# Two-layer block (linear recurrence, then squared-ReLU feed-forward): another order of the VectorE, ScalarE and GpSimd calls of an inner batch

## The chip, the cores and the metric

The kernel runs on one core of one Trainium2 chip. The metric is the device time of one launch in microseconds. It was run three times: 826.71 us median, 822.82 us lowest, 884.32 us highest.

## What is computed

The input is 8 batches of 1024 tokens of width 512, in float32. Cut to what matters:

```
x = x + layernorm(attn(layernorm(x)))
x = x + layernorm(ffn(layernorm(x)))

attn(x):  s    = sigmoid(silu(x @ s_w1.T + s_b1) @ s_w2.T + s_b2)
          u    = (x @ B_w.T + B_b) * s
          h_t  = h_(t-1) @ A.T + u_t            (a scan over the 1024 tokens)
          y    = h @ C_w.T + C_b + x @ D_w.T + D_b
          return y * sigmoid(x @ g_w.T + g_b)
ffn(x):   square(relu(x @ Ws1)) @ Ws2 + routed  (routed is weighted by trunc(softmax weight): 0 unless a weight rounds to 1)
```

## The kernel before

A batch is 128 partitions by 8 tiles j of 128x512. Every operand of a large matmul is split into a high and a low part, and one product is three matmuls (`mm3`, lines 495 to 497: high by high, low by high, high by low). TensorE therefore has, for one inner batch, 396 matmuls of 512 columns, and between them 14 short matmul steps and one step of seven matmuls for the scan (`scan_step`, lines 531 to 539).

All engines run lists of calls written out by hand, one `tail` and one `body` for each batch; the order of the calls on an engine is its program, and engines meet only in semaphores. Batch 0 has a `first_tail`, the batches 1 to 6 a `tail`, the batches 0 to 6 a `body`, and batch 7 a `last_tail` and a `last_body`.

TensorE's `body` of batch b is: Y0 G4 Y1 G5 Y2 G6 Y3 G7 Y4 H00 H01 Y5 B0 SG0 Y6 W1f00 W1f01 Y7 W2(0) W2(1) W2(2) H10 H11 B1 SG1 W2(3). G is the gate of a tile, Y its output, H, B and SG make u of the next batch in two halves, W1f and W2 are the feed-forward in two halves. `tail` holds G0 to G3, the scan, and the second half of the feed-forward of the batch before.

What the prediction follows is the way from Y of a tile to W1f00 of the same batch, which needs tiles 0 to 3:

- VectorE `attn(j)` (line 1307) multiplies Y by the gate; `v_bn`, `v_ag`, `v_ep` (1312, 1316, 1320) take mean and variance; GpSimd `v_rs(j)` (1896) the power -1/2; VectorE `attn_norm(j)` (1324) normalizes.
- GpSimd `x1(j)` (1936) adds the residual. VectorE `x1_bn`, `x1_ag`, `x1_ep` (1329, 1333, 1337), GpSimd `x1_rs(j)` (1896, 1906), ScalarE `x1_norm(j)` (926) are the second norm.
- VectorE `turn(j)` (1347) transposes blocks of 32x32; the transfer queue's `move` (420) moves a pair of tiles by four transfers, after the turns of both; ScalarE `t_hi(j)` (917) and GpSimd `t_low(j)` (1947) split it.
- TensorE `W1f00` waits for `t_low(3)`, and for `u_of(0)` (VectorE, 1381), which frees the PSUM bank that it writes. `u_of(0)` waits for ScalarE's `s_gate(0)` (982), and that for SG0.

Beside it, the next batch's input is normalized on the same engines: a transfer broadcasts the statistics into `rows_in`; ScalarE `rows_apart(m)` (932) spreads a half of them; VectorE `less_mean(i)` and `scaled(i)` (1246) apply them to a pair of tiles; ScalarE `ft_hi(j)` (950) and VectorE `ft_low(j)` (1340) split. TensorE H00 waits for `ft_low(3)`, H10 for `ft_low(7)`. ScalarE `hs(j)` (901) and VectorE `hs_low(j)` (1300) split the state for Y(j). `h1` (1364, 1370) and `h1_low` (1953) make the hidden values that SG takes.

Of the kernel before, what the change touches and what calls it, by code (L numbers as in the profile page):

```python
# [18 lines left out]
def build(nc, x, xt, A, AT, BwT, Bb, CwT, Cb, DwT, Db, s1T, s1b, s2T, s2b, gwT, gb, Ws1p, Ws1, Ws2, W1, W2, Wr, eye, out):  # L19
# [19 lines left out]
    with ExitStack() as ctx:  # L39
# [830 lines left out]
        def _(eng):  # L870
# [128 lines left out]
            def tail(b, rep):  # L999
                a = (b, rep)  # L1000
                hidden(*a, 1, 0)
                gate(*a, 0)
                hidden(*a, 1, 1)
                hs(*a, 0)
                hs(*a, 1)
                gate(*a, 1)
                gate(*a, 2)
                zn(*a, 4)
                zn(*a, 5)
                gate(*a, 3)  # L1010
                zn(*a, 6)
                zn(*a, 7)

            def body(b, rep):
                a = (b, rep)
                hs(*a, 2)
                rows_apart(*a, 0)
                gate(*a, 4)
                ones_in(*a, 0)
                ft_hi(*a, 0)  # L1020
                hs(*a, 3)
# [39 lines left out]
                s_gate(*a, 1)  # L1061
                t_hi(*a, 6)
# [135 lines left out]
        def _(eng):  # L1198
# [276 lines left out]
            def tail(b, rep):  # L1475
# [49 lines left out]
                scan_add(*a, 14)  # L1525

            def body(b, rep):
# [3 lines left out]
                hs_low(*a, 2)  # L1531
# [11 lines left out]
                x1_bn(*a, 0)  # L1543
# [4 lines left out]
                hs_low(*a, 3)
                attn(*a, 2)
                x1_ep(*a, 0)  # L1550
                v_bn(*a, 2)
                x1_bn(*a, 1)
                v_ag(*a, 2)
                x1_ag(*a, 1)
                hs_low(*a, 4)
                x1_ep(*a, 1)
                v_ep(*a, 2)
                ft_low(*a, 2)
                turn(*a, 0)
# [11 lines left out]
                x1_bn(*a, 2)  # L1571
                attn(*a, 4)
                x1_ag(*a, 2)
                x1_ep(*a, 2)
                v_bn(*a, 4)
                x1_bn(*a, 3)
# [3 lines left out]
                v_ep(*a, 4)  # L1580
# [48 lines left out]
                x1_ep(*a, 7)
# [495 lines left out]
```

## Time and profile before

| what | us |
|---|---|
| median of the three runs | 826.71 |
| lowest, highest | 822.82, 884.32 |
| span of the profiled execution | 820.9 |
| TensorE (PE) busy in it | 789.0 |
| GpSimd (POOL) busy | 465.6 |
| VectorE (DVE) busy | 599.7 |
| ScalarE (ACT) busy | 346.7 |
| length of batch 2, first scan step to first scan step | 97.13 |

The page gives the span of the profiled execution, from its first instruction to its last; what lies around the span in that execution is not on the page. A row of a timeline names the start, the length, the engine, the line of the kernel, the operation and its tiles; in brackets stands how long the engine was idle before it and who released it. Times of the prediction are those of batch 2, in us from the start of the span.

### The profile page before, as it was taken

Reading aid. Unit: us, or ns where it says so; the run is one execution under the profiler, and the core shown is the slowest. Engines: PE = TensorE matmul, PEld = TensorE weight load, DVE = VectorE, ACT = ScalarE, POOL = GpSimd, SP = SyncE. Lnnn points to the kernel's source line nnn. Section 1 sums busy time; section 2 is a strip of 40 time slices with the busy share of each in tenths; the row PEclk is TensorE's granted clock in tenths of the full one; section 3 lists DMA queues with packets and bytes.
Section 4 is the critical chain, followed back from the end, with each engine's and each line's share of the span. In section 5 each row is a group of like instructions: output and inputs, shape, how many; then the busy total and the mean of one; then the engine's idle time right before and its main releaser. Section 6 shows DMA issues by size and latency. Waiting matters only on the chain. (4 is left out here: it accounts for less than half of the span.)

```text
span 820.9 us, 10797 instructions
## 1 busy us (share of the span) xinstructions
PE 789.0 (96%) x3644; PEld 650.4 (79%) x3644; DVE 599.7 (73%) x1393; ACT 346.7 (42%) x555; POOL 465.6 (57%) x560
## 2 busy tenths in 40 slices
PE   7989999999999999999999999999999999999985
PEld 6778878887888878888788887888788887888873
DVE  7858875697857977678775787578785797744774
ACT  4524435344433444344433544534443344432453
POOL 1243658438565576456574565844756557634555
PEclk9999999999999999999999999999999999999998
DMA  8524333544255424362334533354425522322112
GB/s 287 175 80 178 95 115 131 177 164 142 81 176 196 139 78 154 110 250 77 100 132 168 192 89 111 137 178 163 145 79 178 188 95 78 102 104 103 52 51 104
DMA packets 39614, 109.85 MB, mean 134 GB/s; under 512 B 6915, under 2 KB 23683, under 8 KB 31750
## 3 DMA queue, kind: packets, MB, share of 16 engines
q1 hardware_dynamic: 39126, 108.95, 39.4%
q8 instruction: 29, 0.48, 0.2%
q10 hardware_dynamic: 432, 0.20, 0.1%
q14 instruction: 27, 0.22, 0.1%
HBM read 60.84 MB, written 33.61 MB: 115 GB/s over the span
## 5 line engine op out<-in xcount | busy, mean ns | idle before, releaser
L1936 POOL TENSOR_TENSOR xres<-work,xres 128x512 f32<-128x512 f32 x64 | 83.1, 1299 | 65.1 <-DVE work L1324 65.1
L1896 POOL TENSOR_TENSOR rsv<-rsv,negh 128x1 f32<-128x1 f32 x64 | 53.3, 832 | 105.9 <-DVE rsv L1320 105.8
L495 PE MATMUL TM<-gw_hi,xT_hi 128*128 128x512 f32 x256 | 107.2, 419 | 0.0
L497 PE MATMUL TM<-gw_hi,xT_lo 128*128 128x512 f32 x256 | 100.7, 393 | 0.0
L497 PE MATMUL TM<-dw_hi,xT_lo 128*128 128x512 f32 x256 | 100.2, 391 | 0.0
L496 PE MATMUL TM<-gw_lo,xT_hi 128*128 128x512 f32 x256 | 100.1, 391 | 0.0
L495 PE MATMUL TM<-dw_hi,xT_hi 128*128 128x512 f32 x256 | 100.0, 391 | 0.0
L496 PE MATMUL TM<-dw_lo,xT_hi 128*128 128x512 f32 x256 | 99.6, 389 | 0.0
L987 ACT ACTIVATE work<-TM,nmz,rsz 128x512 f32<-128x512 f32 x62 | 48.2, 777 | 112.7 <-POOL nmz L1906 112.7
L1940 POOL TENSOR_TENSOR work<-work,xres 128x512 f32<-128x512 f32 x62 | 79.0, 1290 | 8.0 <-ACT work L987 8.0
L1246 DVE TENSOR_TENSOR xin<-xin,norm_row 128x1024 f32<-128x1024 f32 x56 | 71.2, 1305 | 11.4 <-ACT norm_row L932 11.4
L1947 POOL TENSOR_TENSOR x2T_lo<-work,x2T_hi 128x512 fp32r<-128x512 f32 x56 | 70.9, 1288 | 5.8 <-ACT x2T_hi L917 5.8
L926 ACT ACTIVATE work<-xres,nmx,rsx 128x512 f32<-128x512 f32 x64 | 54.5, 871 | 39.7 <-POOL nmx L1906 39.7
L1896 POOL TENSOR_TENSOR mv<-ve,negh 128x4 f32<-128x4 f32 (+1 forms) x17 | 17.9, 1051 | 82.9 <-DVE ve L1221 76.4
L495 PE MATMUL FM<-x2T_hi,f1w_hi 128*128 128x512 f32 x128 | 53.2, 415 | 11.7 <-POOL x2T_lo L1947 11.6
L1307 DVE TENSOR_TENSOR work<-TM,work 128x512 f32<-128x512 f32 x64 | 43.4, 678 | 24.8 <-PE TM L497 24.3
L917 ACT ACTIVATE x2T_hi<-work 128x512 fp32r<-128x512 f32 x56 | 33.7, 625 | 59.4 <-DMA work<-x2q 59.4
L1427 DVE BATCH_NORM_STATS2 st<-TM 128x6 f32<-128x512 f32 x62 | 42.7, 689 | 19.9 <-PE TM L497 19.9
L497 PEld LDWEIGHTS TM<-gw_hi,xT_lo 128*128 128x128 f32 x256 | 48.0, 188 | 10.9
L497 PEld LDWEIGHTS TM<-dw_hi,xT_lo 128*128 128x128 f32 x256 | 48.1, 188 | 10.1
L496 PEld LDWEIGHTS TM<-dw_lo,xT_hi 128*128 128x128 f32 x256 | 48.1, 188 | 9.9
L495 PEld LDWEIGHTS TM<-dw_hi,xT_hi 128*128 128x128 f32 x256 | 48.1, 188 | 9.8
(177 smaller groups left out, 2062.3 us busy)
## 6 DMA issues: line engine op xcount, KB each, us to landing
xres<-in_x SPq DMA_DIRECT2D x16, 1024.0 KB, 5.9
x_scratch<-xres SPq DMA_DIRECT2D x16, 1024.0 KB, 4.6
xin<-in_x SPq DMA_DIRECT2D x15, 1024.0 KB, 5.3
out<-work SPq DMA_DIRECT2D x30, 512.0 KB, 3.4
xin<-in_x_t SPq DMA_DIRECT2D x14, 1024.0 KB, 5.8
work<-x2q SPq DMA_DIRECT2D x112, 128.0 KB, 2.7
rows_in<-ln_scratch SPq DMA_DIRECT2D x14, 512.0 KB, 4.7
xin<-in_x SPq DMA_DIRECT2D x2, 512.0 KB, 5.1
```

The costliest lines, as they stand in the source:

```text
L495: eng.matmul(ps, lhs[0], rhs[0], start=first, stop=False)
L496: eng.matmul(ps, lhs[0], rhs[1], start=False, stop=False)
L497: return eng.matmul(ps, lhs[1], rhs[0], start=False, stop=last)
L926: eng.activation(dst, src, ACT.Identity, bias=nmx[:, j:j + 1], scale=rsx[:, j:j + 1])\
L987: eng.activation(work[:, j, :], z_bank(rep, j)[:, :], ACT.Identity, bias=nmz[:, j:j + 1], scale=rsz[:, j:j + 1]).then_inc(S["zn_ok"], 1)
L1246: return eng.tensor_tensor(xT, xT, r.unsqueeze(2).to_broadcast([P, 2, KD, P]), op)
L1307: eng.tensor_tensor(work[:, j, :], tm_bank(f"y{j}")[:, :], work[:, j, :], ALU.mult)\
L1427: eng.bn_stats(st6[:, 3, j, :], z_bank(rep, j)[:, :]).then_inc(S["z_bn"], 1)
L1896: return eng.tensor_tensor(dst, src, negh[:, 0:n], ALU.pow)
L1936: eng.tensor_tensor(xres[:, j, :], work[:, j, :], xres[:, j, :], ALU.add).then_inc(S["x1_ok"], 1)
L1940: eng.tensor_tensor(work[:, j, :], work[:, j, :], xres[:, j, :], ALU.add).then_inc(S["out_ok"], 1)
L1947: eng.tensor_tensor(by_blocks(x2T_lo[:, j % MS, :, :]), moved_tile(j), by_blocks(x2T_hi[:, j % MS, :, :]).bitcast(F32), ALU.subtract).then ...
```

## The change

The calls of ScalarE's, VectorE's and GpSimd's `tail` and `body` are put in another order. No call is added or taken away, and no call's instructions are changed. TensorE's list and the transfer queue's list stay as they are. `tail` is run by the batches 1 to 6, `body` by the batches 0 to 6.

```diff
 ScalarE, body
+                rows_apart(*a, 0)
                 hs(*a, 2)
-                rows_apart(*a, 0)
                 gate(*a, 4)
...
                 hs(*a, 3)
                 gate(*a, 5)
-                ft_hi(*a, 1)
+                rows_apart(*a, 1)
                 ft_hi(*a, 2)
+                x1_norm(*a, 0)
                 hs(*a, 4)
-                x1_norm(*a, 0)
-                rows_apart(*a, 1)
                 x1_norm(*a, 1)
...
+                t_hi(*a, 2)
+                s_gate(*a, 0)
+                t_hi(*a, 3)
                 hs(*a, 7)
...
 VectorE, body
-                less_mean(*a, 2)
-                turn(*a, 1)
                 attn(*a, 3)
                 v_bn(*a, 3)
+                hs_low(*a, 4)
+                v_ag(*a, 3)
+                less_mean(*a, 3)
+                v_ep(*a, 3)
+                x1_bn(*a, 2)
                 ft_low(*a, 3)
-                v_ag(*a, 3)
-                scaled(*a, 2)
-                v_ep(*a, 3)
-                less_mean(*a, 3)
+                x1_ag(*a, 2)
                 attn_norm(*a, 3)
...
                 turn(*a, 2)
                 h1(*a, 0, 0)
-                x1_ep(*a, 3)
+                turn(*a, 3)
+                x1_bn(*a, 4)
+                x1_ag(*a, 4)
                 h1(*a, 0, 1)
-                x1_bn(*a, 4)
-                turn(*a, 3)
                 attn(*a, 5)
...
 GpSimd, body
                 x1_rs(b, 2)
                 v_rs(b, 4)
+                x1_rs(b, 3)
                 x1(b, 4)
-                x1_rs(b, 3)
+                t_low(b, 1)
                 h1_low(b + 1, 0, 0)
                 h1_low(b + 1, 0, 1)
                 x1_rs(b, 4)
-                t_low(b, 1)
                 v_rs(b, 5)
```

In `tail`, GpSimd takes the second `ln1_rs` earlier, VectorE takes `scan_add(2)` and the statistics of the next input earlier and `hs_low(1)` last, and ScalarE takes `gate(0)` behind `hidden(1,1)` and `hs(0)`.

First place, VectorE in `body` around the turns of tiles 2 and 3. L1347 is a turn (the first of two is tile 2), L1337 the small step `x1_ep`, L1364 and L1370 are `h1`. Before:

```order
L1347 STREAM_TRANSPOSE x2q<-work 128x4x128
L1364 SCALAR_TENSOR_TENSOR hf<-FM0,b_col,hf 128x512
L1370 CAST h1_hi<-hf 128x512
L1337 TENSOR_SCALAR rsx<-mvx 128x1
L1364 SCALAR_TENSOR_TENSOR hf<-FM1,b_col,hf 128x512
L1370 CAST h1_hi<-hf 128x512
L1329 BN_STATS st6<-xres 128x6
L1347 STREAM_TRANSPOSE x2q<-work 128x4x128
```

And now, from `scaled(2)` (L1246) to the turn of tile 3:

```order
L1246 TENSOR_TENSOR xin<-xin,norm_row 128x1024
L1320 TENSOR_SCALAR rsv<-mvv 128x1
L1300 TENSOR_TENSOR hs_lo<-u,hs_hi 128x128
L1337 TENSOR_SCALAR rsx<-mvx 128x1
L1300 TENSOR_TENSOR hs_lo<-u,hs_hi 128x128
L1324 TENSOR_SCALAR work<-work,mvv,rsv 128x512
L1347 STREAM_TRANSPOSE x2q<-work 128x4x128
L1364 SCALAR_TENSOR_TENSOR hf<-FM0,b_col,hf 128x512
L1370 CAST h1_hi<-hf 128x512
L1347 STREAM_TRANSPOSE x2q<-work 128x4x128
```

`x1_ep(3)` stood behind the first `h1` and stands ahead of both turns; the turn of tile 3 stood behind both `h1` and an `x1_bn`, and stands between the two `h1`.

Second place, ScalarE in `body` around the second `rows_apart` (L932). L950 is `ft_hi`, L926 `x1_norm`, L901 `hs`, L892 `gate`. Before:

```order
L901 ACTIVATE hs_hi<-u 128x128
L892 ACTIVATE work<-TM2 128x512
L950 ACTIVATE xT_hi<-xin 128x512 x2
L901 ACTIVATE hs_hi<-u 128x128
L926 ACTIVATE work<-xres,nmx,rsx 128x512
L932 ACTIVATE norm_row<-rows_in 128x1024
L926 ACTIVATE work<-xres,nmx,rsx 128x512
```

And now:

```order
L950 ACTIVATE xT_hi<-xin 128x512 x2
L901 ACTIVATE hs_hi<-u 128x128
L892 ACTIVATE work<-TM2 128x512
L932 ACTIVATE norm_row<-rows_in 128x1024
L950 ACTIVATE xT_hi<-xin 128x512
L926 ACTIVATE work<-xres,nmx,rsx 128x512
L901 ACTIVATE hs_hi<-u 128x128
L926 ACTIVATE work<-xres,nmx,rsx 128x512
```

`rows_apart(1)` stood behind `ft_hi(2)`, `hs(4)` and `x1_norm(0)`, and stands ahead of them.

Third place, ScalarE in `body` from the norm of tiles 2 and 3 (L926) to `s_gate(0)` (L982). L917 is `t_hi`, L972 `sig`. Before, from the norm of tile 3:

```order
L926 ACTIVATE work<-xres,nmx,rsx 128x512
L917 ACTIVATE x2T_hi<-work 128x4x4x32
L892 ACTIVATE work<-TM0 128x512
L901 ACTIVATE hs_hi<-u 128x128
L901 ACTIVATE hs_hi<-carry 128x128
L939 ACTIVATE xin<-xin,one 1x4x128
L950 ACTIVATE xT_hi<-xin 128x512
L917 ACTIVATE x2T_hi<-work 128x4x4x32 x2
L950 ACTIVATE xT_hi<-xin 128x512
L982 ACTIVATE sg<-FM1,b_col 128x512
```

And now, from the norm of tile 2 to `hs(7)` (on carry):

```order
L926 ACTIVATE work<-xres,nmx,rsx 128x512
L917 ACTIVATE x2T_hi<-work 128x4x4x32
L926 ACTIVATE work<-xres,nmx,rsx 128x512
L972 ACTIVATE hf<-FM1,b_col 128x512
L917 ACTIVATE x2T_hi<-work 128x4x4x32
L982 ACTIVATE sg<-FM1,b_col 128x512
L917 ACTIVATE x2T_hi<-work 128x4x4x32
L901 ACTIVATE hs_hi<-carry 128x128
```

`s_gate(0)` stood behind `gate(7)`, two `hs`, `ones_in`, two `ft_hi` and the `t_hi` of tiles 2 and 3, and stands between the `t_hi` of tile 2 and of tile 3.

## Rows read from the trace of the kernel before

**Rows 1.** the page: span, and busy time of the engines

```profile
span 820.9 us, 10797 instructions
...
PE 789.0 (96%) x3644; PEld 650.4 (79%) x3644; DVE 599.7 (73%) x1393; ACT 346.7 (42%) x555; POOL 465.6 (57%) x560
```

**Rows 2.** waits of PE, whole span: line, released by, us in total, times, longest

```profile
PE FM L495 <- POOL x2T_lo L1947: 11.6, 7, 1.9
```

**Rows 3.** windows, batch 2: length, busy us of PE, PEld, DVE, ACT, POOL

```profile
229.23:326.36 97.13, 95.52 (x439) 78.81 (x438) 73.39 (x172) 42.16 (x67) 58.83 (x71) 1.00 0.43 141
```

**Rows 4.** timeline of PE in batch 2: start us, us, engine, line, operation

```profile
283.52 0.40 PE L495 MATMUL FM<-xT_hi,s1w_hi 128*128 128x512 f32 x1
...
296.50 0.39 PE L495 MATMUL TM<-dw_hi,xT_hi 128*128 128x512 f32 x1
...
299.69 0.40 PE L497 MATMUL TM<-cw_hi,hs_lo 128*128 128x512 f32 x1
...
301.70 0.50 PE L495 MATMUL FM<-x2T_hi,f1w_hi 128*128 128x512 f32 x1 [1.61 <-POOL x2T_lo L1947]
...
302.04 0.39 PE L496 MATMUL FM<-x2T_lo,f1w_hi 128*128 128x512 f32 x1
...
314.80 0.39 PE L495 MATMUL FM<-xT_hi,s1w_hi 128*128 128x512 f32 x1
```

**Rows 5.** timeline of VectorE (DVE) in batch 2

```profile
276.50 1.92 DVE L1246 TENSOR_TENSOR xin<-xin,norm_row 128x1024 f32<-128x1024 f32 x1 [0.93 <-ACT norm_row L932]
...
278.97 0.65 DVE L1307 TENSOR_TENSOR work<-TM,work 128x512 f32<-128x512 f32 x1
...
280.26 0.68 DVE L1340 TENSOR_TENSOR xT_lo<-xin,xT_hi 128x512 fp32r<-128x512 f32 x1
...
280.94 1.19 DVE L1246 TENSOR_TENSOR xin<-xin,norm_row 128x1024 f32<-128x1024 f32 x1
...
284.84 0.67 DVE L1307 TENSOR_TENSOR work<-TM,work 128x512 f32<-128x512 f32 x1
...
288.47 0.55 DVE L1324 TENSOR_SCALAR work<-work,mvv,rsv 128x512 f32<-128x512 f32 x1 [0.96 <-POOL rsv L1896]
...
290.67 0.14 DVE L1337 TENSOR_SCALAR rsx<-mvx 128x1 f32<-128x1 f32 x1
...
292.94 0.71 DVE L1347 STREAM_TRANSPOSE x2q<-work 128x512 f32<-128x512 f32 x1 [0.41 <-ACT work L926]
...
300.70 0.75 DVE L1381 SCALAR_TENSOR_TENSOR u<-FM,b_col,sg 128x512 f32<-128x512 f32 x1 [1.58 <-ACT sg L982]
...
313.67 0.68 DVE L1340 TENSOR_TENSOR xT_lo<-xin,xT_hi 128x512 fp32r<-128x512 f32 x1
```

**Rows 6.** timeline of GpSimd (POOL) in batch 2

```profile
276.04 1.29 POOL L1936 TENSOR_TENSOR xres<-work,xres 128x512 f32<-128x512 f32 x1
...
290.89 0.55 POOL L1896 TENSOR_TENSOR rsx<-rsx,negh 128x1 f32<-128x1 f32 x1 [0.43 <-DVE rsx L1337]
...
299.13 2.52 POOL L1947 TENSOR_TENSOR x2T_lo<-work,x2T_hi 128x512 fp32r<-128x512 f32 x2 [0.79 <-ACT x2T_hi L917]
```

**Rows 7.** timeline of ScalarE (ACT) in batch 2

```profile
274.21 2.19 ACT L932 ACTIVATE norm_row<-rows_in 128x1024 f32<-128x1024 f32 x1
...
292.09 0.81 ACT L926 ACTIVATE work<-xres,nmx,rsx 128x512 f32<-128x512 f32 x1 [2.22 <-POOL nmx L1906]
...
298.42 1.15 ACT L917 ACTIVATE x2T_hi<-work 128x512 fp32r<-128x512 f32 x2 [1.35 <-DMA work<-x2q]
...
300.00 0.67 ACT L982 ACTIVATE sg<-FM,b_col 128x512 f32<-128x512 f32 x1
```

**Rows 8.** timeline of the transfer queue (SP) in batch 2

```profile
267.18 0.32 SPq L412 DMA_DIRECT2D rows_in<-ln_scratch  x1
...
293.68 2.50 SPq L420 DMA_DIRECT2D work<-x2q  x4
```

**Rows 9.** the tile rows_in, whole span: its transfers

```profile
DMA to landing us min/median/max: 3.5/4.7/6.0
```

More of the change, by code:

```diff
@@ L1009, in tail @@
                 zn(*a, 5)
+                hs(*a, 1)
                 gate(*a, 3)
@@ L1061, in body @@
                 s_gate(*a, 1)
+                t_hi(*a, 5)
                 t_hi(*a, 6)
@@ L1524, in tail @@
                 z_ep(*a, 7)
-                scan_add(*a, 14)
+                hs_low(*a, 1)
             def body(b, rep):
@@ L1542, in body @@
                 v_ag(*a, 1)
[L1543 removed]
+                hs_low(*a, 2)
                 v_ep(*a, 1)
                 ft_low(*a, 1)
+                x1_bn(*a, 0)
                 attn_norm(*a, 1)
+                hs_low(*a, 3)
                 x1_ag(*a, 0)
[L1548 removed]
+                x1_ep(*a, 0)
                 attn(*a, 2)
[L1550 removed]
+                x1_bn(*a, 1)
+                x1_ag(*a, 1)
+                x1_ep(*a, 1)
                 v_bn(*a, 2)
[L1552 removed]
+                less_mean(*a, 2)
                 v_ag(*a, 2)
[L1554 to L1556 removed]
+                turn(*a, 0)
                 v_ep(*a, 2)
                 ft_low(*a, 2)
[L1559 removed]
+                turn(*a, 1)
                 attn_norm(*a, 2)
[L1561 to L1562 removed]
                 attn(*a, 3)
                 v_bn(*a, 3)
+                hs_low(*a, 4)
[3 more added lines that the diff above has]
+                x1_bn(*a, 2)
                 ft_low(*a, 3)
[L1566 to L1569 removed]
+                x1_ag(*a, 2)
                 attn_norm(*a, 3)
[L1571 removed]
+                x1_ep(*a, 2)
                 attn(*a, 4)
[L1573 to L1574 removed]
+                x1_bn(*a, 3)
                 v_bn(*a, 4)
[L1576 removed]
                 x1_ag(*a, 3)
                 v_ag(*a, 4)
+                scaled(*a, 2)
+                v_ep(*a, 4)
                 hs_low(*a, 5)
[L1580 removed]
+                x1_ep(*a, 3)
+                hs_low(*a, 6)
                 attn_norm(*a, 4)
@@ L1594, in body @@
                 v_ep(*a, 5)
-                hs_low(*a, 6)
+                scaled(*a, 3)
                 attn_norm(*a, 5)
+                u_of(*a, 0)
+                turn(*a, 4)
                 hs_low(*a, 7)
-                u_of(*a, 0)
                 attn(*a, 6)
                 v_bn(*a, 6)
-                turn(*a, 4)
                 x1_bn(*a, 5)
+                x1_ag(*a, 5)
+                x1_ep(*a, 5)
                 v_ag(*a, 6)
-                x1_ag(*a, 5)
                 v_ep(*a, 6)
-                x1_ep(*a, 5)
                 ft_low(*a, 4)
@@ L1609, in body @@
                 attn_norm(*a, 6)
+                ft_low(*a, 5)
                 turn(*a, 5)
@@ L1616, in body @@
                 v_bn(*a, 7)
-                z_bn(*a, 0)
                 v_ag(*a, 7)
-                x1_ep(*a, 6)
                 ft_low(*a, 6)
                 v_ep(*a, 7)
+                x1_ep(*a, 6)
+                z_bn(*a, 0)
                 ft_low(*a, 7)
+                attn_norm(*a, 7)
                 z_bn(*a, 1)
-                attn_norm(*a, 7)
                 z_ag(*a, 0)
+                z_bn(*a, 2)
+                x1_bn(*a, 7)
+                z_ag(*a, 1)
                 z_ep(*a, 0)
-                x1_bn(*a, 7)
                 x1_ag(*a, 7)
+                z_ag(*a, 2)
                 x1_ep(*a, 7)
+                z_ep(*a, 1)
+                turn(*a, 6)
                 h1(*a, 1, 0)
-                z_ag(*a, 1)
-                turn(*a, 6)
-                z_ep(*a, 1)
                 turn(*a, 7)
                 h1(*a, 1, 1)
-                z_bn(*a, 2)
+                z_ep(*a, 2)
                 u_of(*a, 1)
-                z_ag(*a, 2)
                 z_bn(*a, 3)
                 z_ag(*a, 3)
-                z_ep(*a, 2)
                 z_ep(*a, 3)
@@ L1977, in body @@
                 x1_rs(b, 0)
+                x1_rs(b, 1)
                 v_rs(b, 2)
-                x1_rs(b, 1)
                 x1(b, 2)
@@ L1995, in body @@
                 x1(b, 5)
+                x1_rs(b, 5)
                 v_rs(b, 6)
-                x1_rs(b, 5)
                 x1(b, 6)
@@ L2001, in body @@
                 x1(b, 7)
+                x1_rs(b, 7)
                 z_rs(b, 0)
-                x1_rs(b, 7)
                 h1_low(b + 1, 1, 0)
```

78 lines of the change are left out of this document (35 added, 43 removed).

## The prediction

> **What bounds the kernel now.** I read the page first: TensorE is busy for 789.0 of 820.9 us [rows 1], so nothing that makes another engine quicker pays unless TensorE waits for it. Then the waits of TensorE: one line carries nearly all of them, the first matmul of W1f released by GpSimd's `t_low` (x2T_lo), 11.6 us in seven waits, the longest 1.9 [rows 2]. Seven is the number of `body` calls, batches 0 to 6. Then one batch by itself: from scan to scan 97.13 us pass, and TensorE is busy 95.52 of them [rows 3]. The missing 1.61 is exactly the one wait before W1f00 at 301.70 [rows 4]. So an inner batch has no other TensorE gap to win, and all that a new order can give is these seven waits; what it can take is open.
>
> How much one wait costs: the last matmul of Y6 starts at 299.69, W1f00 at 301.70 [rows 4], 2.01 us. The usual step from matmul to matmul is 0.23 (from 296.50 to 299.69 are 14 steps). So 1.78 are lost, and the step behind the wait is 0.34 (301.70 to 302.04), 0.11 more: 1.89 in all, 0.28 above the idle time that the row shows. Seven waits: 11.6 + 7 x 0.28 = 13.6 us.
>
> Back from W1f00 along the timelines: `t_low` of tiles 2 and 3 ends at 301.65 [rows 6]; it waited for `t_hi` at 298.42, which waited for the transfers [rows 7]; these were issued from 293.68 [rows 8], when `turn(3)`, started at 292.94, was done [rows 5]; the turn waited for `x1_norm(3)` at 292.09 [rows 7], that for GpSimd's `x1_rs(3)` at 290.89 [rows 6], and that for `x1_ep(3)` at 290.67 [rows 5]. `x1_ep(3)` is 0.14 long and had its input long before: it stood in VectorE's list behind `attn_norm(4)`, `turn(2)` and the first `h1`. That is the place where the order makes the wait. Beside it, `u_of(0)` started at 300.70 and ended at 301.45 [rows 5], because `s_gate(0)` came at 300.00 [rows 7]; W1f00 waits for it too, so an earlier `t_low` alone would have won only 0.2.
>
> **The change part by part.** *VectorE, up to `x1_ep(3)`.* `scaled(2)` (1.19 at 280.94) leaves the place ahead of `attn_norm(3)` and `attn(4)`, so `attn(4)`, at 284.84 before, can start at 283.65; Y4 ends when H00 starts, at 283.52 [rows 4, 5], so it may. From there to `x1_ep(3)` now stand: `attn(4)` 0.67, two statistics of a full tile (0.7 each, as the other full-tile rows), `scaled(2)` 1.19, and five small steps of about 0.15 to 0.2: 4.1 us. `x1_ep(3)` comes at 287.8 instead of 290.67.
>
> *To `turn(3)`.* From `x1_ep(3)` to the start of `x1_norm(3)` it was 1.42, from there to the turn 0.85 [rows 5, 7]. GpSimd now has `x1_rs(3)` ahead of `x1(4)`, so its queue does not add to that. The turn could start at 290.1. VectorE has `attn_norm(4)`, `turn(2)` and one `h1` ahead of it; these three took from 288.47 to 290.67 [rows 5], and `attn_norm(4)` hangs on GpSimd, so I leave it where it was. The turn then starts between 290.1 and 290.7, 2.2 to 2.8 us earlier; I take 2.2.
>
> *To W1f00.* The transfers, `t_hi(2)` and `t_low` follow the turn: `t_hi(2)` at 296.2, the end of `t_low(3)` at 299.45. The 0.67 of `s_gate(0)` between the two `t_hi` is hidden by `t_low(2)`, 1.26 long (half of 2.52). `s_gate(0)` waits for SG0, which ends at 296.50 [rows 4]; with 0.67 for it and 0.75 for `u_of(0)` the bank is free at about 298.2. TensorE wants W1f00 at 299.69 + 0.23 = 299.92. Both are there, `t_low(3)` with a lead of 0.5 (1.1 with the turn at 290.1), `u_of(0)` with 1.7. The wait goes: -13.6 us. What is late next is `t_low(3)` itself, by that small lead.
>
> *`rows_apart(1)` and `ft_low(3)`.* This is where the change takes time from something that was in time. `rows_apart(1)` (2.19) now stands on ScalarE ahead of `ft_hi(2)`, `x1_norm(0)`, `hs(4)` and `x1_norm(1)`, and on VectorE `less_mean(2)`, which waits for it, ahead of `v_ag(2)`, both turns of the first pair, `attn_norm(2)` and `attn(3)`. Its rows were issued at 267.18 [rows 8]; transfers of this kind land after 3.5 to 6.0 [rows 9]; ScalarE took them at 274.21 before [rows 7], so the trace does not show when they were there. With 3.5 they are there at 270.7 and spread at 272.9; then 1.92 (the dear one of rows 5), two turns 1.42, `ft_low(2)` 0.68, `attn_norm(2)` 0.55 and small steps 0.5 put `attn(3)` at 278.0, 1.0 ahead of its 278.97. To the end of `ft_low(3)` it was 1.97 (278.97 to 280.94); now `hs_low(4)`, `less_mean(3)` and an `x1_bn` come between, some 2.2 more: 282.2. H00 wants it at 283.52 [rows 4]. Lead 1.3, cost nothing; with a landing of 6.0 the loss is 1.2 for a batch, 8 us in all. I take nothing, by the middle of the row (4.7), where 0.1 of lead is left.
>
> *`ft_low(7)`.* It ends at 314.35 for H10 at 314.80 [rows 4, 5], a lead of 0.45; the same calls lie between `attn(7)` and it, in another order. Bounds: nothing, or one full-tile step of 0.68 too much, 0.23 x 7 = 1.6. Together with the 0.5 at `t_low(3)` I take 0.1 for a batch, 0.8 in all.
>
> *The calls in `tail`*, and all others that move, are covered by TensorE's own work: in rows 3 nothing but the one wait is left, so each had some lead. Bounds: no gain; a lead lost costs at most one full-tile step, 0.7 x 6 = 4 us. I take nothing. The transfer queue's list stays; the only call ahead of the second pair on it, the load of a later input, hangs on `ft_low(3)` at 282.2, and the pair comes at 291.4.
>
> Sum: 820.9 - 13.6 + 0.8 = 808.1 us of span. What lies around the span in that execution is not shown; the two lower runs stand 1.9 and 5.8 above it, the middle is 3.9. Forecast 812.0, 1.8% under the median of 826.71.
>
> **One shared port.** `less_mean(2)` took 1.92 at 276.50, where the same operation took 1.19 at 280.94 [rows 5]; GpSimd ran `x1(2)`, a full tile, from 276.04 to 277.33 [rows 6], and 277.33 + 1.19 is just where it ended. So it waited for GpSimd to finish. The Trainium skill, "SBUF — State Buffer", section "Who interferes with whom", says that a VectorE instruction with two SBUF inputs contends with a GpSimd instruction that reads SBUF, and that whoever issues first has the shared ports for the whole instruction; this trace agrees, with 0.73 lost. The first rival prices what that does here, from the rows alone.
>
> **The rivals.** *The wait shrinks but stays* (0.17). `scaled(2)` and two `hs_low` now lie between `attn(4)` and the turn, each with two SBUF inputs, while GpSimd runs `x1(3)` and `t_low(0)`. Each can lose 0.73 as in rows 5 and 6, up to 1.29. Three times 0.73 is 2.2; less the lead of 0.5 to 1.1 this leaves 1.1 to 1.7 of the 1.78. For it: the new neighbours are real. Against it: VectorE idled in this stretch (0.96 and 0.41, rows 5), which takes up a part. The idle takes up about 0.7 of it, so that half the gain is left: 818.
>
> *No change* (0.08). `t_hi(2)` now stands ahead of `s_gate(0)`: if the pair lands late, `u_of(0)` is late with it, and W1f00 waits for that instead. At a landing 2 us later than I have it both are back at 301.5. Time 825.
>
> *Slower* (0.09). The rows for `rows_apart(1)` land late. From a landing of 4.8 on, H00 waits for `ft_low(3)`; with 1.89 more (6.7) the whole gain is gone. At 8 H00 is 3.2 late, 7 x 3.2 = 22 less 13.6, some 834. Slower by 2% needs about 9 us. Against it: the row's longest is 6.0.
>
> **How the numbers follow.** Forecast 0.66, by itself 809 to 815 (the two distances around the span, and the bounds at `ft_low(7)`). The range of 808 to 824 takes in the second case and most of the leads lost in `tail`; it leaves out the slow case and half of the unchanged. About 2% (16.5 us) is what a measurement of this kernel can tell from no change. The seven waits are 13.6 us, under it, so faster by more than 2% needs luck in what lies around the span: 0.08. Slower by more than 2% is a third of the slow case, 0.03. Within 2%: 0.89.
>
> **What would show it.** In the waits of TensorE after, the line of W1f released by `t_low` is gone or under 2 us, and no line of H (`ft_low`), Y or the scan takes its place; a batch is 95.2 to 95.6 long from scan to scan. `turn(3)` starts at least 2 us earlier against Y6, and `s_gate(0)` lies between the two `t_hi`. I am wrong if W1f00 still waits for more than 0.5 in most batches, or if H00 or H10 waits.

## The result, and the profile after

The changed kernel takes 808.55 us in the median of four runs (807.87 to 809.46); the kernel before, with one more run beside them, 825.58 (822.82 to 884.32). The ratio, which leaves the slow execution of 884.32 us out, is 0.9819, with a 95% interval of 0.9802 to 0.9836. The forecast was 812.0 us, within a range of 808 to 824, and "within 2%" with a chance of 0.89: 1.8% is what came. The profiled execution took 809.22 us, and the page gives its span and the engines' busy time:

```profile
span 807.4 us, 10797 instructions
...
PE 786.8 (97%) x3644; PEld 650.9 (81%) x3644; DVE 601.0 (74%) x1393; ACT 347.3 (43%) x555; POOL 465.1 (58%) x560
```

Against [rows 1] the span is 13.5 shorter, and TensorE is busy for 2.2 less although it does the same matmuls; the 0.28 that the prediction puts on top of each wait would make 1.96 of them. The waits of TensorE (line, released by, us in total, times, longest) tell where the time went:

```profile
PE TR L573 <- ACT work L926: 2.2, 1, 2.2
PE TR L515 <- ACT apt L880: 1.8, 5, 0.4
```

These two head the list now, and both have the same length in the kernel before. The row of [rows 2], W1f released by `t_low` (x2T_lo), is gone, and no row of H, Y or the scan has taken its place. The window of batch 2, first scan step to first scan step, in the columns of [rows 3]:

```profile
225.58:320.81 95.23, 95.23 (x440) 78.89 (x438) 73.46 (x172) 41.91 (x67) 58.77 (x71) 1.00 0.44 144
```

95.23 long instead of 97.13, and TensorE is busy through all of it. Three places of TensorE's timeline in that batch, the starts of H00, of Y6 and of W1f00 (behind the last matmul of Y6), none with a wait in brackets:

```profile
279.86 0.40 PE L495 MATMUL FM<-xT_hi,s1w_hi 128*128 128x512 f32 x1
...
292.84 0.39 PE L495 MATMUL TM<-dw_hi,xT_hi 128*128 128x512 f32 x1
...
296.03 0.39 PE L497 MATMUL TM<-cw_hi,hs_lo 128*128 128x512 f32 x1
296.26 0.40 PE L495 MATMUL FM<-x2T_hi,f1w_hi 128*128 128x512 f32 x1
```

What had to be there, on VectorE: `ft_low(3)`, `x1_ep(3)`, `turn(3)`, `attn_norm(5)` and `u_of(0)`:

```profile
277.29 0.67 DVE L1340 TENSOR_TENSOR xT_lo<-xin,xT_hi 128x512 fp32r<-128x512 f32 x1
...
283.45 0.15 DVE L1337 TENSOR_SCALAR rsx<-mvx 128x1 f32<-128x1 f32 x1
...
286.52 0.70 DVE L1347 STREAM_TRANSPOSE x2q<-work 128x512 f32<-128x512 f32 x1
...
292.82 1.52 DVE L1324 TENSOR_SCALAR work<-work,mvv,rsv 128x512 f32<-128x512 f32 x1 [0.67 <-POOL rsv L1896]
294.27 0.74 DVE L1381 SCALAR_TENSOR_TENSOR u<-FM,b_col,sg 128x512 f32<-128x512 f32 x1
```

On GpSimd `x1_rs(3)`, now ahead of `x1(4)` (L1936), and the two `t_low`:

```profile
283.94 0.65 POOL L1896 TENSOR_TENSOR rsx<-rsx,negh 128x1 f32<-128x1 f32 x1
284.79 0.26 POOL L1906 TENSOR_SCALAR nmx<-mvx,rsx 128x1 f32<-128x1 f32 x1 [0.20 <-POOLq L1902]
285.02 1.29 POOL L1936 TENSOR_TENSOR xres<-work,xres 128x512 f32<-128x512 f32 x1
...
292.77 1.29 POOL L1947 TENSOR_TENSOR x2T_lo<-work,x2T_hi 128x512 fp32r<-128x512 f32 x1
294.33 1.29 POOL L1947 TENSOR_TENSOR x2T_lo<-work,x2T_hi 128x512 fp32r<-128x512 f32 x1 [0.27 <-ACT x2T_hi L917]
```

And on ScalarE `rows_apart(1)`, then `t_hi(2)`, `s_gate(0)` and `t_hi(3)`:

```profile
267.03 2.26 ACT L932 ACTIVATE norm_row<-rows_in 128x1024 f32<-128x1024 f32 x1 [2.11 <-DMA rows_in<-ln_scratch]
...
292.06 0.63 ACT L917 ACTIVATE x2T_hi<-work 128x512 fp32r<-128x512 f32 x1 [5.58 <-DMA work<-x2q]
293.04 0.69 ACT L982 ACTIVATE sg<-FM,b_col 128x512 f32<-128x512 f32 x1 [0.35 <-PE FM L675]
293.63 0.62 ACT L917 ACTIVATE x2T_hi<-work 128x512 fp32r<-128x512 f32 x1
```

`t_low(3)` ends at 295.62, 0.64 ahead of W1f00; `u_of(0)` at 295.01, 1.25 ahead; `ft_low(3)` at 277.96, 1.90 ahead of H00. In the row of `t_hi(2)` ScalarE stands idle for 5.58 before it, released by the transfers: they alone hold this call now, and `turn(3)` holds them; no call in ScalarE's list stands in its way any more.

### The profile page after: what moved, and what is told of

Read it like the earlier page. It is cut to its first block and busy times, and to the rows that moved or that the text cites. A ratio compares the mean times of both kernels' runs of the same rounds, so it can differ in the third digit from the quotient of the medians.

```text
span 807.4 us, 10797 instructions
## 1 busy us (share of the span) xinstructions
PE 786.8 (97%) x3644; PEld 650.9 (81%) x3644; DVE 601.0 (74%) x1393; ACT 347.3 (43%) x555; POOL 465.1 (58%) x560
## 5 line engine op out<-in xcount | busy, mean ns | idle before, releaser
L1936 POOL TENSOR_TENSOR xres<-work,xres 128x512 f32<-128x512 f32 x64 | 85.4, 1334 | 63.3 <-DVE work L1324 63.3
L495 PE MATMUL TM<-gw_hi,xT_hi 128*128 128x512 f32 x256 | 107.2, 419 | 0.0
L495 PE MATMUL TM<-dw_hi,xT_hi 128*128 128x512 f32 x256 | 100.1, 391 | 0.0
L1896 POOL TENSOR_TENSOR rsv<-rsv,negh 128x1 f32<-128x1 f32 x64 | 46.4, 725 | 76.6 <-DVE rsv L1320 76.5
L1947 POOL TENSOR_TENSOR x2T_lo<-work,x2T_hi 128x512 fp32r<-128x512 f32 x56 | 72.9, 1313 | 1.9 <-ACT x2T_hi L917 1.9
L1896 POOL TENSOR_TENSOR rsz<-rsz,negh 128x1 f32<-128x1 f32 x64 | 36.5, 570 | 58.4 <-DVE rsz L1435 57.8
L1246 DVE TENSOR_TENSOR xin<-xin,norm_row 128x1024 f32<-128x1024 f32 x56 | 66.1, 1211 | 1.0 <-ACT norm_row L932 0.9
L926 ACT ACTIVATE work<-xres,nmx,rsx 128x512 f32<-128x512 f32 x64 | 55.2, 872 | 25.7 <-POOL nmx L1906 25.7
L1896 POOL TENSOR_TENSOR rsx<-rsx,negh 128x1 f32<-128x1 f32 x64 | 40.6, 634 | 32.4 <-DVE rsx L1337 32.4
L917 ACT ACTIVATE x2T_hi<-work 128x512 fp32r<-128x512 f32 x56 | 33.7, 626 | 54.7 <-DMA work<-x2q 54.7
L495 PEld LDWEIGHTS TM<-dw_hi,xT_hi 128*128 128x128 f32 x256 | 48.1, 188 | 9.8
L892 ACT ACTIVATE work<-TM 128x512 f32<-128x512 f32 x64 | 37.2, 591 | 42.5 <-PE TM L497 37.5
```

The costliest lines, as they stand in the source:

```text
L495: eng.matmul(ps, lhs[0], rhs[0], start=first, stop=False)
L892: eng.activation(work[:, j, :], tm_bank(f"g{j}")[:, :], ACT.Sigmoid).then_inc(S["gate_ok"], 1)
L926: eng.activation(dst, src, ACT.Identity, bias=nmx[:, j:j + 1], scale=rsx[:, j:j + 1])\
L1246: return eng.tensor_tensor(xT, xT, r.unsqueeze(2).to_broadcast([P, 2, KD, P]), op)
L1896: return eng.tensor_tensor(dst, src, negh[:, 0:n], ALU.pow)
L1936: eng.tensor_tensor(xres[:, j, :], work[:, j, :], xres[:, j, :], ALU.add).then_inc(S["x1_ok"], 1)
```

## The experiments

The first six put the change into the kernel before piece by piece, each on top of the one ahead, to see which piece carries the gain. Then one piece is taken out of the changed kernel, one cost is put in, the `tail` functions are tried alone, and one call of the last batch is moved. In every kernel but that of the late rows all calls are the same, in another order.

**Step 1: VectorE alone.** `x1_ep(3)` is put ahead of `attn_norm(4)`, `turn(3)` between the two `h1`.

```diff
+                x1_ep(*a, 3)
                 attn_norm(*a, 4)
                 turn(*a, 2)
                 h1(*a, 0, 0)
-                x1_ep(*a, 3)
+                turn(*a, 3)
                 h1(*a, 0, 1)
                 x1_bn(*a, 4)
-                turn(*a, 3)
```

> The kernel before, with VectorE's list alone mended in body: x1_ep(3) ahead of attn_norm(4), and turn(3) between the two h1. Theory: the wait before W1f00 is held by three lists, not by one. GpSimd still has x1_rs(3) behind x1(4), which ended at 290.45 in the trace before, and t_low(2) behind x1_rs(4), t_low(1) and v_rs(5), which ended at 298.34 against the 299.13 at which t_low(2) started; so at most 0.8 us of a batch goes, 7 x 0.8 = 5.6 us, and W1f00 still waits 0.8 to 1.6 each time, released by t_low. Rival (the prediction's wording, that x1_ep(3)'s place in VectorE's list is what makes the wait): most of the 13.6 us goes with this edit, 10 us or more.

Measured: 843.28 us, 2.33% slower than before (ratio 1.0233, 1.0214 to 1.0252). The waits of TensorE, then VectorE's `turn(3)` in batch 2, then a window of TensorE behind W1f00, then its first matmuls there:

```profile
PE FM L495 <- DVE u L1381: 22.4, 8, 3.0
```

```profile
300.02 0.71 DVE L1347 STREAM_TRANSPOSE x2q<-work 128x512 f32<-128x512 f32 x1 [1.76 <-ACT work L926]
```

```profile
310.72:317.87 7.15, 7.15 (x24) 5.76 (x25) 5.20 (x13) 1.94 (x3) 2.16 (x4) 0.76 0.01 2
```

```profile
310.72 0.56 PE L495 MATMUL FM<-x2T_hi,f1w_hi 128*128 128x512 f32 x1 [3.00 <-DVE u L1381]
311.08 0.63 PE L496 MATMUL FM<-x2T_lo,f1w_hi 128*128 128x512 f32 x1
311.50 0.63 PE L497 MATMUL FM<-x2T_hi,f1w_lo 128*128 128x512 f32 x1
...
314.44 0.39 PE L495 MATMUL FM<-x2T_hi,f1w_hi 128*128 128x512 f32 x1
314.67 0.39 PE L496 MATMUL FM<-x2T_lo,f1w_hi 128*128 128x512 f32 x1
```

Neither the theory (up to 5.6 us won) nor the rival (10 us or more) came: the kernel lost 19.9. `turn(3)` was moved ahead of what it waits for: on GpSimd `x1_rs(3)` was still behind `x1(4)`, so VectorE stood still for 1.76 with its whole list behind it, and `u_of(0)` became the last to come. Two of the steps ahead of it were dear as well: `attn_norm(5)` took 1.50 and `hs_low(7)` 1.34, where they took 0.55 and 0.29 before; step 2 shows beside what. The wait grew from some 1.6 to 3.0.
**Step 2: GpSimd's `x1_rs(3)` as well.**

```diff
                 v_rs(b, 4)
+                x1_rs(b, 3)
                 x1(b, 4)
-                x1_rs(b, 3)
```

> As s1_vector, and GpSimd's x1_rs(3) ahead of x1(4). Theory: turn(3) now comes about 2 us earlier, but t_low(2) stays held in GpSimd's list until 298.3; still 4 to 7 us won over the kernel before, W1f00 waits about 0.8 each time. Rival (only the norm of tile 3 is late): 11 us or more, the wait is gone.

Measured: 822.66 us, ratio 0.9988 (0.9977 to 0.9998): the loss of step 1 is gone and next to nothing is won, where the theory had 4 to 7 us and the rival 11. TensorE's waits; VectorE in batch 2, from `attn_norm(5)` over `hs_low(7)` to `u_of(0)`; GpSimd's two `t_low`; and last `attn_norm(5)` and `hs_low(7)` in batch 2 of the kernel before:

```profile
PE FM L495 <- DVE u L1381: 13.0, 8, 1.7
```

```profile
298.32 1.51 DVE L1324 TENSOR_SCALAR work<-work,mvv,rsv 128x512 f32<-128x512 f32 x1 [0.45 <-POOL rsv L1896]
299.75 1.36 DVE L1300 TENSOR_TENSOR hs_lo<-carry,hs_hi 128x128 fp32r<-128x128 f32 x1
301.03 0.74 DVE L1381 SCALAR_TENSOR_TENSOR u<-FM,b_col,sg 128x512 f32<-128x512 f32 x1
```

```profile
298.25 2.71 POOL L1947 TENSOR_TENSOR x2T_lo<-work,x2T_hi 128x512 fp32r<-128x512 f32 x2
```

```profile
298.37 0.55 DVE L1324 TENSOR_SCALAR work<-work,mvv,rsv 128x512 f32<-128x512 f32 x1 [0.44 <-POOL rsv L1896]
...
298.83 0.29 DVE L1300 TENSOR_TENSOR hs_lo<-carry,hs_hi 128x128 fp32r<-128x128 f32 x1
```

`turn(3)` came 1.95 earlier against Y6, as the prediction wanted, and W1f00 waits as long as before, for `u_of(0)` now. Ahead of it on VectorE `attn_norm(5)` took 1.51 and `hs_low(7)`, a 128x128 step, 1.36; each ran against one of the two `t_low` on GpSimd. In the kernel before the two `t_low` start at 299.13 [rows 6], behind both steps, and these take 0.55 and 0.29. That is the first rival of the prediction, at calls that it didn't name.

**Step 3: GpSimd's `t_low(1)` ahead of both `h1_low`.**

```diff
                 x1(b, 4)
+                t_low(b, 1)
                 h1_low(b + 1, 0, 0)
                 h1_low(b + 1, 0, 1)
                 x1_rs(b, 4)
-                t_low(b, 1)
```

> As s2_vector_gpsimd_rs, and GpSimd's t_low(1) ahead of both h1_low. ScalarE's list is that of before. Theory: s_gate(0) was late only because it stood behind the two t_hi that waited for the pair; with the pair 2 us earlier it comes at 298 and u_of(0) ends at 299.3, before the 299.92 at which TensorE wants it, so the wait is gone or under 0.5: 10 to 13.6 us won. Rival (the prediction's wording, that an earlier t_low alone wins only 0.2 of a batch because of u_of(0)): 1.4 us won, and TensorE's wait is put down to u_of(0).

Measured: 816.92 us, ratio 0.9920 (0.9903 to 0.9937). The wait is 0.9 in each of seven batches, released by `t_low` again: `PE FM L495 <- POOL x2T_lo L1947`, 6.2 us. 6.4 us are won, neither the 10 or more of the theory nor the 1.4 of the rival, and somewhat under half of the whole gain.

**Step 4: ScalarE's `s_gate(0)` between the two `t_hi`.**

```diff
                 t_hi(*a, 2)
+                s_gate(*a, 0)
                 t_hi(*a, 3)
                 ft_hi(*a, 5)
-                s_gate(*a, 0)
```

> As s3_vector_gpsimd, and ScalarE's s_gate(0) between t_hi(2) and t_hi(3): five calls moved in all. Theory: 12 to 13.6 us won over the kernel before, as much as by the whole change, TensorE without a wait before W1f00. Rival (the rest of the change is needed too, as scaled(2) behind attn(4) or rows_apart(1)): less than 10 us.

Measured: 816.55 us, ratio 0.9923 (0.9906 to 0.9941): no change from step 3. TensorE's wait, ScalarE from `ones_in(1)` to `t_hi(2)` in batch 2, and VectorE's `scaled(3)`:

```profile
PE FM L495 <- POOL x2T_lo L1947: 6.3, 7, 0.9
```

```profile
294.95 0.72 ACT L939 ACTIVATE xin<-xin,one 1x512 f32<-1x512 f32 x1 [3.40 <-DVE xin L1246]
295.70 0.63 ACT L950 ACTIVATE xT_hi<-xin 128x512 fp32r<-128x512 f32 x1
296.24 0.61 ACT L917 ACTIVATE x2T_hi<-work 128x512 fp32r<-128x512 f32 x1
```

```profile
292.81 2.10 DVE L1246 TENSOR_TENSOR xin<-xin,norm_row 128x1024 f32<-128x1024 f32 x1
```

`t_hi(2)` stands behind `ones_in(1)`, a call for the next batch, and that waited 3.40 for `scaled(3)`. So the theory fell; the rival's time (less than 10 us) came, but this holder is none of the calls that it named. The changed kernel has `ones_in(1)` and `ft_hi(4)` behind both `t_hi`.

**Step 5: so `ones_in(1)` and `ft_hi(4)` behind `t_hi(3)`.**

```diff
-                ones_in(*a, 1)
-                ft_hi(*a, 4)
                 t_hi(*a, 2)
                 s_gate(*a, 0)
                 t_hi(*a, 3)
+                ones_in(*a, 1)
+                ft_hi(*a, 4)
```

> The kernel before, with the fourth step's edits and, on ScalarE, ones_in(1) and ft_hi(4) moved behind t_hi(3). Theory (the last holder of t_hi(2) is ones_in(1), which waits for scaled(3) on VectorE): the seven waits at W1f00 go or fall under 0.2 us each; 809 to 812 us, ratio 0.982 to 0.986, as the changed kernel. Rival (u_of(0) or t_low(3) is late through the shared port, as after the second step): a wait of 0.4 to 0.9 us stays in each batch, 813 to 817 us.

Measured: 821.07 us, ratio 0.9981 (0.9966 to 0.9997), some 4.5 us slower than step 4. The theory fell, and the rival was itself too small. TensorE's wait; VectorE in batch 2; GpSimd:

```profile
PE FM L495 <- DVE u L1381: 11.7, 8, 1.5
```

```profile
298.77 1.50 DVE L1324 TENSOR_SCALAR work<-work,mvv,rsv 128x512 f32<-128x512 f32 x1 [0.47 <-POOL rsv L1896]
300.20 1.37 DVE L1300 TENSOR_TENSOR hs_lo<-carry,hs_hi 128x128 fp32r<-128x128 f32 x1
```

```profile
298.70 2.71 POOL L1947 TENSOR_TENSOR x2T_lo<-work,x2T_hi 128x512 fp32r<-128x512 f32 x2
```

Because `t_hi` now comes in time, GpSimd starts its `t_low` at 298.70, 0.07 ahead of `attn_norm(5)`, which takes 1.50; in step 4 it started behind it, and `attn_norm(5)` took 0.55. The wait of step 2 is back: `u_of(0)` pays for the earlier `t_low`.

**Step 6: VectorE's `scaled(3)` later, `u_of(0)` ahead of `hs_low(7)`.**

```diff
-                scaled(*a, 3)
                 v_bn(*a, 5)
                 v_ag(*a, 5)
                 v_ep(*a, 5)
                 hs_low(*a, 6)
+                scaled(*a, 3)
                 attn_norm(*a, 5)
-                hs_low(*a, 7)
                 u_of(*a, 0)
+                hs_low(*a, 7)
```

> The kernel before, with the fifth step's edits and, on VectorE, scaled(3) put behind v_ep(5) and u_of(0) right behind attn_norm(5), ahead of hs_low(7). Theory (what was left after the fifth step is VectorE's order around u_of(0): hs_low(7) and scaled(3) standing against GpSimd's full-tile work): u_of(0) is done 1.0 to 1.4 us earlier, the wait at W1f00 falls from 1.46 to 0.3 or less, 809 to 813 us, ratio 0.982 to 0.988. Rival (the shared port takes it back at another call, attn_norm(5) or t_low(3)): 0.5 to 1.0 us stays in each batch, released by t_low(3), 814 to 818 us.

Measured: 810.13 us (809.15 to 812.62), ratio 0.9831 (0.9815 to 0.9846); the changed kernel, run again beside it, 808.17 (807.57 to 809.47), ratio 0.9815 (0.9799 to 0.9831). TensorE's wait at W1f00:

```profile
PE FM L495 <- POOL x2T_lo L1947: 1.8, 2, 0.9
```

The time is the theory's (809 to 813): the wait is gone in five of seven batches and 0.9 in the first two. So nine calls moved in three lists carry 13.3 of the 15.2 us that the change gives against the 823.39 of the kernel before, measured beside them; the 1.8 us of the two waits that stay are about what is left. Which of the two moves of this step does it was not tried.

**The place of `x1_ep(3)`, taken back in the changed kernel.**

```diff
-                x1_ep(*a, 3)
                 hs_low(*a, 6)
                 attn_norm(*a, 4)
                 turn(*a, 2)
                 h1(*a, 0, 0)
+                x1_ep(*a, 3)
                 turn(*a, 3)
```

> The changed kernel with one call put back: x1_ep(3) on VectorE behind the first h1, right ahead of turn(3), as in the kernel before. Theory (this place alone makes the wait, in the new order too): x1_ep(3) and turn(3) come about 2 us later, t_hi(2) and t_low(3) with them; less the lead of 0.64, W1f00 waits 1.3 to 1.9 us in each batch, +9 to +14 us against the changed kernel (818 to 823). Rival (the three lists hold it together, and GpSimd and VectorE have slack behind the turn): under 0.7 us for a batch, 809 to 813 us. Slower than the kernel before if VectorE stands still at turn(3), as in the first step.

Measured: 821.82 us, ratio 0.9985 (0.9976 to 0.9995). Putting back one call of 0.15 us takes all but 1 us of the gain. TensorE's waits, and VectorE's `turn(3)`:

```profile
PE FM L495 <- POOL x2T_lo L1947: 5.9, 7, 0.9
...
PE FM L675 <- POOL h_lo L1953: 2.1, 7, 0.3
```

```profile
292.03 0.71 DVE L1347 STREAM_TRANSPOSE x2q<-work 128x512 f32<-128x512 f32 x1 [1.99 <-ACT work L926]
```

The time is the theory's (818 to 823), but the wait at W1f00 is less than it said (0.84 instead of 1.3 to 1.9). VectorE stands still at `turn(3)` for 1.99, so what stands behind it is late too, and SG0, which takes what `h1_low` makes, waits for 0.3. A batch is some 97.0 long instead of 95.23; the two waits, each with the 0.28 of the prediction on top, make 1.7 of these 1.8.

**Late rows.** `rows_apart(1)` in the changed kernel, written three times.

```diff
+                for _ in range(more):
+                    again[0] += 1
+                    eng.activation(norm_row[:, m, :, :], rows_in[:, :, :].rearrange("p c s -> p s c"), ACT.Copy)\
+                       .then_inc(spread, 1)
+                    eng.wait_ge(spread, again[0])
...
-                rows_apart(*a, 1)
+                rows_apart(*a, 1, 2)
```

> The changed kernel with rows_apart(1) written three times instead of once on ScalarE (2.26 us each, so the spread rows come 4.5 us later; the result is the same). Tests the slower rival of the prediction: late rows make H00 wait for ft_low(3). With the lead of 1.9 us that the trace of the changed kernel shows, H00 waits 2.0 to 2.6 us in each of seven batches, released by ft_low: +14 to +20 us against the changed kernel, 823 to 829 us, no faster than the kernel before. If VectorE makes up part of it behind less_mean(2), or the lead is really larger: +4 to +10 us. If ScalarE is late instead with x1_norm(0) and t_hi(0), the wait is at W1f or at T and not at H00.

Measured: 822.69 us, ratio 0.9992 (0.9978 to 1.0007). TensorE's wait at H00 (this kernel's line numbers are 1 to 8 higher), and the two added copies in batch 2:

```profile
PE FM L496 <- DVE xT_lo L1348: 8.0, 6, 1.4
```

```profile
270.09 4.45 ACT L937 ACTIVATE norm_row<-rows_in 128x1024 f32<-128x1024 f32 x2 [2.25 <-DMA rows_in<-ln_scratch]
```

The slower rival of the prediction is a real mechanism, at the place that it named: with the rows 4.45 later H00 waits 1.23 to 1.38 in the batches 1 to 6 (2.0 to 2.6 in seven were expected), W1f00 is some 0.3 late as well, and the whole gain goes. It is just not what these rows do. In the changed kernel the rows came 3.6 to 4.0 after they were issued in the batches 1 to 6, 3.6 in batch 2, and `ft_low(3)` has 1.90 to spare at that.

**The `tail` functions alone**, in the kernel before; a part of the edit, first of ScalarE, then of VectorE:

```diff
-                gate(*a, 0)
                 hidden(*a, 1, 1)
                 hs(*a, 0)
-                hs(*a, 1)
+                gate(*a, 0)
...
                 scan_add(*a, 1)
+                scan_add(*a, 2)
+                l1_bn(b + 1, 2)
                 l1_ag(b + 1, 0)
```

> The kernel before with only the three tail functions of the changed kernel (the calls between two batches); the bodies stay. Theory (only the seven waits in the bodies count): the same time within 1 us of the kernel before, and the seven waits at W1f00 still there, 11 to 12 us. Rival (the tails carry part of the gain by what they hand to the next body): 2 to 6 us faster.

Measured: 822.60 us against 822.78, ratio 0.9984 (0.9969 to 0.9999), and 11.8 us in seven waits at W1f00. The `tail` functions give nothing by themselves. The bodies without them were not run; step 6, which leaves the `tail` functions as they were, has 13.3 of the 15.2 us.

**The wait that is left, in the last batch.** The longest wait of the changed kernel is 2.2 us, in the last batch at T(5) (there TensorE itself transposes a tile, line 573), for `x1_norm(5)`; its input was there at 772.90, and ScalarE sat idle until 773.80 for `hidden(0,1)`, which stood ahead of it.

```diff
-                hidden(*a, 0, 1)
                 x1_norm(*a, 5)
+                hidden(*a, 0, 1)
                 t_hi(*a, 4)
```

> The changed kernel with one call moved in the last batch: on ScalarE x1_norm(5) ahead of hidden(0,1). In the trace of the changed kernel x1_norm(5) had its input at 772.9, ScalarE stood idle until 773.80 for hidden(0,1), and T(5) on TensorE waited 2.2 us for x1_norm(5), with slower matmuls behind the wait. Theory: the 2.2 us go, 0.7 to 1 comes back at W2(0) or T(7), which are late next: 806 to 807.5 us, 1 to 3 us under the changed kernel. Rival (the chain through x1_norm(7) and t_low(7) sets the end of this stretch): the same time within 0.5 us.

And the changed kernel beside it:

> The changed kernel once more, beside the other two on the same chip, so that they can be compared with it: 807 to 810 us, ratio to the kernel before 0.980 to 0.984.

Measured: 807.29 us, 807.22 to 807.41 in five runs, ratio 0.9799 (0.9784 to 0.9813), against 808.17, 807.57 to 809.47. The intervals of the two ratios overlap; the five times of the one all lie below the five of the other. The wait of 2.2 shrank to 0.2, and one at W2(0) came in its place, for the `h_lo` of `hidden(0,1)`:

```profile
PE TM L495 <- DVE h_lo L1400: 1.2, 1, 1.2
```

This kernel is the fastest of all that were run, by 0.9 us in the median. The lowest times of the two are only 0.35 apart; a part of the 0.9 comes from the two executions of the changed kernel at 809.25 and 809.47, whose clock was lower (last section).

## Why the prediction was right, point by point

- *What bounds the kernel, and how much the wait is worth.* Right. The seven waits were the only gap; the profiled spans differ by 13.5 us, where the prediction had 13.6 less 0.8. The 0.8 for small leads lost did not come: TensorE has no gap in the window of batch 2, and the batches 1 to 5 are all 95.23 long.
- *One wait costs 1.89.* Right for six of seven (the six batches differ by 1.71 to 1.96), wrong for batch 3. From scan to scan the changed kernel takes 95.23, the one before 97.13 in batch 2, 1.90 more. But the kernel before takes 99.03 in its batch 3, 3.80 more: the wait there is the longest, 1.94, and behind it the clock fell:

```profile
399.13 0.50 PE L495 MATMUL FM<-x2T_hi,f1w_hi 128*128 128x512 f32 x1 [1.94 <-POOL x2T_lo L1947]
...
401.06 0.63 PE L496 MATMUL FM<-x2T_lo,f1w_hi 128*128 128x512 f32 x1
401.49 0.63 PE L497 MATMUL FM<-x2T_hi,f1w_lo 128*128 128x512 f32 x1
```

  The prediction read the price above the idle time, 0.28, in one batch and took it seven times; that left some 1.6 us of slower matmuls out of the sum. In the changed kernel's profiled execution 1.5 were lost in the last batch in the same way (last section). That the two cancel, and the sum of 13.6 stands against 13.5, is luck.
- *The place where the order makes the wait.* Right as far as it goes, and too narrow. Step 1 shows that `x1_ep(3)` and `turn(3)` moved alone lose 20 us; the changed kernel with `x1_ep(3)` put back shows that without its new place the rest of the change is worth 1 us. The wait was held at the same time by VectorE's list (`x1_ep(3)`, `turn(3)`, `scaled(3)`, `hs_low(7)` ahead of `u_of(0)`), by GpSimd's (`x1_rs(3)` behind `x1(4)`, `t_low(1)` behind `h1_low`) and by ScalarE's (`ones_in(1)` ahead of `t_hi(2)`). For `s_gate(0)` there is only the trace of before, where it came at 300.00; step 4, which moved it while `t_hi(2)` was still late, changed nothing. The prediction named four of these (`x1_ep(3)`, `turn(3)`, `x1_rs(3)`, `s_gate(0)`), and of `u_of(0)` it said that an earlier `t_low` alone wins only 0.2; step 2 shows nothing won.
- *`turn(3)` 2.2 to 2.8 earlier; I took 2.2.* It started 3.56 ahead of Y6 before and starts 6.32 ahead of it now: 2.76, the upper end. The prediction left `attn_norm(4)` where it was; it came 0.8 earlier against Y6 (8.83 ahead of it instead of 8.03). And `x1_ep(3)` came 3.56 earlier, not 2.9: from `attn(4)` to it were 3.4, where the prediction added up 4.1. `t_low(3)` has a lead of 0.64 (0.5 predicted), `u_of(0)` of 1.25 (1.7 predicted). The end of `t_low(3)` gained less than the turn, 2.37 against Y6, since `s_gate(0)`, now between the two `t_hi`, waited 0.35 for SG0, and `t_low(3)` 0.27 for `t_hi(3)`.
- *`ft_low(3)`, lead 1.3.* It is 1.90, and the late rows show that a delay of 4.45 loses about the whole gain. The 0.09 for this rival was spent on a landing (6.7) that these rows don't have.
- *The shared port, 0.17.* The rival's mechanism is real and dear, but at `attn_norm(5)` and `hs_low(7)`, not at `scaled(2)`, which took 1.19, nor at the two `hs_low` ahead of the turn, which took 0.28 each. In the changed kernel `attn_norm(5)` still takes 1.52, and is still in time, since `u_of(0)` stands right behind it and `hs_low(7)` behind that. The prediction says nothing of that place, and its 1.7 for the lead of `u_of(0)` has no such 1.52 in it. So there was luck in "gone": with `hs_low(7)` ahead of `u_of(0)`, 1.37 in step 5, the lead of 1.25 would be used up. And `less_mean(2)` of [rows 5] did not end "just where" the sum puts it: that is 278.52, the row ends at 278.42.
- *812.0 against 808.55.* 0.7 of the 3.4 us is the span (808.1 predicted, 807.4 here). The rest is what lies around the span: 3.9 was taken, between two runs of before; 1.8 is what the changed kernel's profiled run has (809.22 less 807.4), and every execution whose span is known, of either kernel, has 1.7 to 1.9. So the 3.9 was no distance around a span; the two runs that it came from were longer by themselves. The remaining 0.7 is between the profiled run and the median. The forecast's share came out, 1.8%, because its base, 826.71, was high by about as much as the forecast: beside the later runs the kernel before has medians of 822.78 to 823.39. That is luck too.

## What to carry to other kernels

A wait that shows one releaser can be held by several lists at once: walk back each of its inputs, and reckon for each what is late next when the first is gone. A call moved ahead of what it waits for blocks all that stands behind it in its list, so an order must be changed on all engines of a chain together; two of VectorE's moves alone were 2.3% slower than none. When a GpSimd step is made earlier, look which VectorE step with its tiles in SBUF it now meets, and put the call that TensorE wants ahead of it.

## What the runs showed of the hardware

**A wait of about 2 us can cost two thirds more than its length.** In the changed kernel's profiled execution the 2.21 of the last batch are followed by 1.5 of slower matmuls; from its first scan step to the end that batch takes 104.34 there, and 102.82 in the second run of the same kernel, where the clock did not fall. TensorE's window behind the wait of 2.21 in the last batch (length, busy times, granted clock third from the end), first in the changed kernel's profiled execution, then in that of its second run:

```profile
776.41:779.74 3.33, 3.33 (x11) 2.81 (x11) 1.11 (x4) 2.49 (x4) 1.08 (x3) 0.52 0.68 280
```

```profile
776.19:779.42 3.23, 3.23 (x16) 2.67 (x17) 2.27 (x7) 2.85 (x4) 1.08 (x3) 1.00 0.71 292
```

With a granted clock of 0.52 the matmuls are 0.43 apart (1.2 GHz), with 1.00 0.23 (2.4 GHz), behind the same wait. The Trainium skill, "TensorE: Matmul & The Clock Gate", section "Part 1: The HAM clock gate", says that an idle array falls to half its clock and that work brings it back; the steps agree, 0.43 and 0.23. Twelve of the traces have this wait: in six the last batch takes 104.3 to 104.5, in the other six 102.8 to 102.9. The five runs of the second time have a mean clock of 0.996 at 807.57, 807.77 and 808.17 us, and of 0.994 at 809.25 and 809.47. The kernel without that wait stays within 0.2 us. In step 1, where the waits are 3.0, the clock fell at all seven, and the fall cost 1.7 us in batch 2 (7.15 against 5.46), beside the wait. What decides in one and the same kernel whether it falls was not tried.

The kernel before, with its seven waits more, scatters in the same steps: of 31 executions five took 820.9 to 821.2 us at a mean clock of 0.995 to 0.996, twenty 822.3 to 823.3 at 0.993 to 0.994, four 824.5 to 824.9 at 0.992, and two 826.1 and 826.6 at 0.990. At 0.995 to 0.996 the changed kernel, in other sets, takes 807.6 to 808.2: some 13.2 us less, and seven times 1.89 is 13.2. That the medians measured side by side are 15.2 apart would then be the clock, which falls more seldom where there are fewer waits; this split is an estimate from these times and clocks, no experiment made it.

**GpSimd's full-tile steps hold VectorE's, small ones too.** `attn_norm(5)` took 1.50 to 1.52 beside a `t_low` and 0.55 without, and `hs_low(7)` 1.36 and 1.37 where it takes 0.29 without. In the changed kernel `attn_norm(5)` ends at 294.34, 0.28 behind the end of `t_low(2)`: it seems to have waited for that, though not with all of its 0.55. It goes the other way too: in step 2 GpSimd's power -1/2 for `x1_rs(4)` took 1.46 beside VectorE's `scaled(3)`, which had started 0.16 ahead of it, and 0.55 in [rows 6]. A step with one of its two tiles in PSUM was not held: `attn(4)` took 0.67 at 284.84 [rows 5] while GpSimd ran `x1(3)`, 1.29 from 284.40. The Trainium skill, "SBUF — State Buffer", section "Who interferes with whom", lets two kinds of VectorE step contend: those with two inputs in SBUF, as `hs_low`, and those with one that run in a mode with both ports, for which it names `tensor_scalar`, as `attn_norm`. The trace agrees with both in that they were held; that `attn_norm` runs in that mode is not shown by it.
